# Softmax sums of a two-layer model: three quarters of the keys added by DMA onto the first quarter's weights, and one product with ones per head pair on four column tiles

## The reference, cut to what matters

```python
q = (x @ Wq + bq).reshape(B, S, H, DK)          # S = 512, H = 16, DK = 64
k = x @ Wk + bk
v = x @ Wv + bv
scores = jnp.einsum('bshd,btd->bhst', q, k) / np.sqrt(DK).astype(x.dtype)
w = jax.nn.softmax(scores, axis=-1)
out = jnp.einsum('bhst,btd->bshd', w, v).reshape(B, S, H * DV)
return out @ Wo + bo
```

## Time and profile before

| | us |
|---|---|
| median of 3 runs | 1349.38 |
| lowest, highest | 1345.81, 1350.87 |
| the profiled execution | 1346.94 |
| its span in the trace | 1345.2 |
| TensorE busy (matmul) | 1233.3 |
| VectorE busy | 1011.2 |
| ScalarE busy | 683.2 |
| GpSimd busy | 263.2 |

### The profile page before, as it was taken

The page is one execution under the profiler, slowest core; times in us unless marked ns, Lnnn a source line. Parts: engine busy times, 40 slices in busy tenths (PEclk is TensorE's granted clock), DMA queues, the critical chain, the costliest instruction groups (busy, mean ns, idle before and its releaser), DMA issues.

```text
span 1345.2 us, 21825 instructions
## 1 busy us (share of the span) xinstructions
PE 1233.3 (92%) x7185; PEld 725.0 (54%) x7185; DVE 1011.2 (75%) x2393; ACT 683.2 (51%) x1252; POOL 263.2 (20%) x314
## 2 busy tenths in 40 slices
PE   4559999999999999999999999999999989998997
PEld 2335445554555455555555555455555458785843
DVE  7776888578857885788588857886796767686775
ACT  3126545544554455444644464446444468685741
POOL 2033222200120012001200120012000206372640
PEclk9659999999999999999999999999999999998998
DMA  2062665122312231224222321232121457474461
GB/s 78 0 174 69 193 200 179 49 63 56 115 36 63 65 116 38 52 67 100 64 50 55 115 65 50 49 120 65 50 50 49 131 173 232 153 238 137 150 214 55
DMA packets 89779, 133.80 MB, mean 99 GB/s; under 512 B 33293, under 2 KB 49229, under 8 KB 85701
## 3 DMA queue, kind: packets, MB, share of 16 engines
q1 hardware_dynamic: 75108, 99.80, 26.2%
q0 software_dynamic: 11344, 31.64, 7.1%
q10 hardware_dynamic: 3216, 0.97, 0.3%
HBM read 59.86 MB, written 38.68 MB: 73 GB/s over the span
## 4 chain that ended last, share of the span: by engine, by line
PE 69%; DVE 19%; issue 4%; ACT 3%; SPq 3%; DMA 2%; POOL 1%; DVEq 0%; ACTq 0%; POOLq 0%
PE bank L1466 14%; PE bank L1438 7%; PE bank L1477 6%; PE bank L1392 6%; PE bank L1439 5%; PE bank L1297 4%; PE bank L1498 4%; PE bank L1299 4%; PE bank L1298 4%; DVE mneg L1029 4%; DVE q_lm L1021 3%; PE bank L1313 2%; PE bank L1348 2%; PE bank L1303 2%; PE bank L1356 1%
## 5 line engine op out<-in xcount | busy, mean ns | idle before, releaser
L846 ACT ACTIVATE wide<-bank 128x512 f32<-128x512 f32 x512 | 294.9, 598 | 338.2 <-PE bank L1439 337.8
L1029 DVE TENSOR_REDUCE mneg<-bank 128x1 f32<-128x512 f32 x512 | 329.7, 684 | 136.0 <-PE bank L1392 130.8
L1466 PE MATMUL bank<-wide,v_w 128*32 128x512 f32 x2048 | 246.2, 598 | 1.3 <-issue 1.0
L1438 PE MATMUL bank<-q_hh,k_hl 128*128 128x512 f32 x512 | 233.0, 455 | 11.3 <-ACT wide L846 11.3
L1439 PE MATMUL bank<-q_lm,k_h 65*128 65x512 f32 x512 | 203.1, 397 | 0.0
L1438 PEld LDWEIGHTS bank<-q_hh,k_hl 128*128 128x128 f32 x512 | 96.3, 188 | 131.6 <-issue 76.9
L636 POOL TENSOR_TENSOR rs<-rs,power 128x4 f32<-128x4 f32 x24 | 24.5, 1020 | 640.2 <-DVE rs L920 640.1
L1477 PE MATMUL bank<-wide,ones 128*32 128x512 f32 x992 | 129.1, 592 | 0.0
L708 POOL DMA_INDIRECT y_rows<-y_m,to_u x92 | 98.9, 1075 | 126.8 <-DVE y_m L1155 102.3
L1466 PEld LDWEIGHTS bank<-wide,v_w 128*32 128x32 f32 x2048 | 53.5, 109 | 121.0 <-issue 112.1
L1392 PE MATMUL bank<-k_b,q_x 128*128 128x512 f32 x256 | 104.4, 408 | 9.7 <-ACT qk L742 6.2
(11 more groups left out here) (238 smaller groups left out, 1969.8 us busy)
## 6 DMA issues: line engine op xcount, KB each, us to landing
q_hh<-q_x SPq DMA_DIRECT2D x256, 128.0 KB, 2.4
w_t<-w_rows SPq DMA_DIRECT2D x23, 1024.0 KB, 4.7
x_rows<-part_h POOLq DMA_DIRECT2D x65, 258.0 KB, 5.0
inv<-inverse_scratch SPq DMA_DIRECT2D x124, 128.0 KB, 2.9
w_rows<-w_t SPq DMA_DIRECT2D x8, 1024.0 KB, 5.0
x_m<-x_rows SPq DMA_DIRECT2D x23, 258.0 KB, 3.9
stage<-in_L_ffn_W SPq DMA_DIRECT2D x16, 256.0 KB, 5.0
yab<-y_rows POOLq DMA_DIRECT2D x8, 512.0 KB, 7.9
```

The source lines that it names most:

```text
L846: act.activation(wide[:, st.g % WIDE, :], ps, ACT.Exp, scale=SCALE1).then_inc(wide_full, 1)
L1029: dve.tensor_reduce(mneg[:, pair % 2, col:col + 1], ps[:], X, ALU.max, negate=True).then_inc(free, 1)
L1438: pe.matmul(ps, k_hl[:, n, t], q_hh[:, gh % HEADS, :], start=True, stop=False)
L1466: pe.matmul(ps_out[0][rows, :], v_w[:, n, c, TILE * d:TILE * d + TILE], weights, start=(c == 0), stop=(c == TT - 1))
```

## The change

Pairs 0 to 53 (`added(pair)`, `ADDED` = 54) form their sums in another way; pairs 54 to 63 stay as they were. For an added pair:

- ScalarE takes the exponential of the first key quarter twice, once into `wide` and once into a new buffer `total` (two buffers of both heads, 2 x 512 columns). The signal `wide_full` comes with the second.
- GpSimd issues three DMAs that add the slots of quarters 1, 2 and 3 (both heads, 128 x 1024 fp32, 512 KB) onto `total`. Each waits for the exponentials of its quarter and for the completion of the add before it.
- TensorE no longer multiplies the weights with ones. Instead `sum_of_added` runs four products of `ones` with 256 columns of `total`, one for each head and half of the queries on its own column tile, at the start of the next pair's first `values`.
- ScalarE may fill a slot of `wide` of quarters 1 to 3 again only once its add has landed, and `total` only once the pair two before has been summed.
- `sraw` is copied three steps later and over 256 columns only; the store of the sums, the reciprocal and the multiplication move two steps later (`SUM_LATER`), the second half of the output projection too (`WO_AT`). The addition L1209 goes.
- GpSimd's program is written along the steps: `root`, the adds, `split_expert`, the single scatters and the single zeroing DMAs each have a step number. Two of VectorE's cuts of layer 0 move (`L0_DVE`).
- `part_h` and `total` share their storage; `zeros` becomes a tensor of its own.

The diff, cut to its core:

```diff
+    ADDED = (NB - 1) * (H // 2) - 2
+    ADD_AT = {4: 1, 6: 2, 8: 3}
+    SUM_LATER = 2
+    WO_AT = [ATT - 10, ATT + 20]
...
-    L0_DVE = [-14, -11, -11, -10, -7, -6, -4, -2, 0, 0, 9, 10, 13, 17, 18, 21, 25, 26, 29, 30, 30, 31, 32,
-              34, 35, 37, 38, 39, 40, 42, 43, 44, 44]
+    L0_DVE = [-14, -13, -11, -10, -7, -6, -4, -2, 0, 0, 9, 10, 13, 17, 18, 21, 25, 26, 29, 30, 30, 32, 32,
+              34, 35, 37, 38, 39, 40, 42, 42, 44, 44]
...
+    ROOT_AT = [30, 42, 51]
+    SCATTER_AT = [[3, 5, 7, 9], [17, 19, 21, 23]]
+    ZERO_AT = [25 + 2 * e for e in range(E)]
...
+    def on_sum(st):
+        return st.kind == "o" and added(pair_of(st)) and head_at(st.k)[1] == 0
+    def adds_before(pair, c):
+        return (TT - 1) * pair + c
...
+            def add(pair, c):
+                g = ATT * (pair // (H // 2)) + PAIR * (pair % (H // 2))
+                pool.wait_ge(wide_full, g + 2 * c + 2)
+                if pair or c > 1:
+                    pool.wait_ge(add_done, adds_before(pair, c - 1) * 16)
+                i = wide_at[g + 2 * c]
+                pool.dma_start(total[:, pair % 2], wide[:, i:i + 2, :], accum_op=ALU.add).then_inc(add_done, 16)
...
+            for st in steps:
+                if st.kind != "o":
+                    continue
+                if st.r < NB - 2 and st.k in ROOT_AT or st.r == NB - 2 and st.k in ROOT_AT[0:2]:
                     root()
+                if add_event(st) is not None:
+                    add(*add_event(st))
+                if st.r == 0 and st.k in SPLIT_STEPS:
+                    split_expert(SPLIT_STEPS.index(st.k))
...
-                    if st.g >= WIDE:
-                        act.wait_ge(second_done, st.g - WIDE + 1)
+                    past = wide_before.get(st.g)
+                    if past is not None:
+                        act.wait_ge(second_done, past.g + 1)
+                        if past.kind == "o" and added(pair_of(past)) and not on_sum(past):
+                            act.wait_ge(add_done, adds_before(pair_of(past), head_at(past.k)[1]) * 16)
...
+                        ins = act.activation(wide[:, wide_at[st.g], :], ps, ACT.Exp, scale=SCALE1)
+                        if on_sum(st):
+                            if pair_of(st) >= 2:
+                                act.wait_ge(summed, pair_of(st) - 1)
+                            ins = act.activation(total[:, pair_of(st) % 2, st.k % 2, :], ps, ACT.Exp, scale=SCALE1)
+                        ins.then_inc(wide_full, 1)
...
+                pair = pair_end(st, 4)
+                if pair is not None and added(pair):
+                    act.wait_ge(summed, pair + 1)
+                    act.wait_ge(sums_stored[pair % 2], 16 * (pair // 2))
+                    act.activation(sraw[:, pair % 2, 0:S // 2], ps_out[1][:, 0:S // 2], ACT.Identity).then_inc(out_free[1], 1)
...
+            def sum_of_added(pair):
+                free_bank(("ps", pair))
+                pe.wait_ge(add_done, adds_before(pair, TT - 1) * 16)
+                for b in range(2):
+                    for h in range(2):
+                        rows, cols = slice(DK * b + TILE * h, DK * b + TILE * h + TILE), slice(S // 2 * h, S // 2 * h + S // 2)
+                        last = pe.matmul(ps_out[1][rows, 0:S // 2], ones[:], total[:, pair % 2, b, cols], start=True, stop=True)
+                last.then_inc(summed, 1)
...
                 if half == 0:
+                    if pair and added(pair - 1):
+                        sum_of_added(pair - 1)
+                    free_bank(("pv", pair))
...
+                        if added(pair):
+                            last.then_inc(second_done, 1)
+                if added(pair):
+                    return
```

More of the change, by code:

```diff
@@ L183, in pair_end, with add_event @@
         return past.r * (H // 2) + past.k // PAIR
+    def add_event(st):
+        if st.kind != "o":
+            return None
+        for at_, c in ADD_AT.items():
+            pair, s = divmod(ATT * st.r + st.k - at_, PAIR)
+            if s == 0 and 0 <= pair and added(pair):
+                return pair, c
+        return None
     def direct(pair):
@@ L241, in norm_at @@
     def norm_at(r):
-        at_ = dict(enumerate(NORM_AT))
+        at_ = {p: k + (SUM_LATER if added(r * (H // 2) + p) else 0) for p, k in enumerate(NORM_AT)}
         if r == NB - 1:
@@ L402, in two_layers @@
         lo_done, second_done = sem("lo_done"), sem("second_done")
+        add_done, summed = sem("add_done"), sem("summed")
         out_free = [sem(f"out_free{i}") for i in range(OUTB)]
@@ L508, in sums_and_inverses @@
                         continue
-                    if k == PAIR * p + 12:
+                    later = SUM_LATER if added(pair) else 0
+                    if k == PAIR * p + 12 + later:
                         emptied(sp, ("ps", pair))
@@ L518, in sums_and_inverses @@
                         sp.wait_ge(inverted, four)
-                        sp.dma_start(sums[:], scratch_s.rearrange("a g (p n) -> (g p) a n", p=32)).then_inc(sums_loaded, 16)
-                    if k == PAIR * p + 17 and p % 2 == 1:
+                        if added(pair):
+                            sp.dma_start(sums[:, 0, :], scratch_s[0].rearrange("g (p n) -> (g p) n", p=32)).then_inc(sums_loaded, 16)
+                        else:
+                            sp.dma_start(sums[:], scratch_s.rearrange("a g (p n) -> (g p) a n", p=32)).then_inc(sums_loaded, 16)
+                    if k == PAIR * p + 17 + later and p % 2 == 1:
                         for i in range(2):
@@ L655, in _, with zero, scatter @@
                     .then_inc(split_l, 1)
-            pool.memset(part_h[:].bitcast(F32), 0.0).then_inc(consts, 1)
+            pool.memset(zeros[:], 0.0).then_inc(consts, 1)
             pool.memset(k_a[:].bitcast(F32), 0.0).then_inc(consts, 1)
             pool.memset(k_b[:].bitcast(F32), 0.0).then_inc(consts, 1)
[L661 to L670, removed]
+            def zero(n, e):
+                pool.dma_start(x_rows[ZONE * e + S * n:ZONE * e + S * (n + 1), :].rearrange("(p i) c -> p (i c)", p=P),
+                               zeros[:]).then_inc(zeroed[n % 2], 16)
+            def scatter(n, b, i):
+                if i == 0:
                     if n or b:
@@ L678, in scatter, with split_expert @@
                         pool.wait_ge(routed, n + 1)
[L679 to L691, removed]
+                pool.indirect_dma_start(x_rows, bass.IndirectOffsetOnAxis(ap=slot_u[:, b, i:i + 1], axis=0),
+                                        xr[:, i, :], None).then_inc(scattered, 16)
+            def split_expert(j):
                 e, second = divmod(j, 2)
@@ L1206, in row_end @@
                     pair = r * (H // 2) + p
-                    if k == PAIR * p + 16 and not direct(pair):
+                    if k == PAIR * p + 16 + (SUM_LATER if added(pair) else 0) and not direct(pair):
                         dve.wait_ge(sums_loaded, 16 * (pair // 2 + 1))
-                        link(dve.tensor_tensor(sums[:, 0, :], sums[:, 0, :], sums[:, 1, :], ALU.add))
+                        if not added(pair):
+                            link(dve.tensor_tensor(sums[:, 0, :], sums[:, 0, :], sums[:, 1, :], ALU.add))
                         dve.reciprocal(sums[:, 0, :], sums[:, 0, :]).then_inc(inverted, 1)
@@ L1473, in values @@
                                 rows = slice(DK * b + TILE * d, DK * b + TILE * d + TILE)
-                                last = pe.matmul(ps_out[1][rows, :], ones[:], weights, start=(c == 0), stop=(c == TT - 1))
+                                last = pe.matmul(ps_out[1][rows, :], ones[:], weights_of(c, b), start=(c == 0), stop=(c == TT - 1))
                         else:
                             rows = slice(DK * b + TILE * (c % 2), DK * b + TILE * (c % 2) + TILE)
-                            last = pe.matmul(ps_out[1][rows, :], ones[:], weights, start=(half == 0), stop=(half == 1))
+                            last = pe.matmul(ps_out[1][rows, :], ones[:], weights_of(c, b), start=(half == 0), stop=(half == 1))
                         last.then_inc(second_done, 1)
```

95 lines of the change are left out of this document (66 added, 29 removed).

## The result

The changed kernel takes 1455.6 us (median of 4 runs, 1449.3 to 1462.6), the kernel before 1348.2: a ratio of 1.080 (1.074 to 1.085). It is 107 us slower, where 31 us faster was forecast. The number is that of rival A (1452 at L = 6.0); the mechanism, as the experiments show, is for the most part another.

The account below looks back on a forecast made before the run. TensorE, busy for 92% of the span, was taken as the bound. 1346.9 - 70.2 (TensorE) + 10.5 (VectorE) + 21 + 8 (adds) = 1316.2 us, as a median 1318; likeliest case 1300 to 1333, 8 in 10 within 1284 to 1400.

Parts of the forecast that it names:

- rival A: The adds in series bound nearly all pairs; slower from L of about 5.3, 1452 us at L = 6.0; chance 0.29.
- L: Time on GpSimd from one add's issue to the next one's; taken as 4.6 us, 5.2 in batch 0.
- What TensorE is rid of: TensorE loses two groups of products with ones and gains a half: net 1.30 us a pair, 70.2 us over the run.
- ScalarE's second exponential: Two more exponentials a pair on ScalarE, hidden in time; taken as even, bound 16 us either way.
- VectorE's 1.5 us a batch: VectorE, nearly full in the fourth and fifth pair, gives back some gain: 10.5 us for seven batches.
- The chain of adds: Three GpSimd adds in series per pair hold up light pairs: 21 us in batches 1 to 6, 8 in batch 0.
- The double pass: An add passes its data twice through the DMA engines: 1.7 + 3.2 = 4.9 us, against 3.3 priced as a copy.
- the prediction's own formula: A pair lasts at least 3L, nothing carried over between pairs; at 13.8 us, 3.5 us lost a batch.
- the prediction's own signs: In the profile after, A shows L above 5.3, batches over 137 us, ScalarE's add waits nearly everywhere, perhaps a lower clock.
- these adds are alone in their queue by construction: Reason for keeping L near 2.4 to 4.9 us, not the 7.9 of a DMA with seven like it around.
- 0.5 us for the others' traffic on the adds: Added to the middle price of 4.1 us for query copies and zeroing DMAs, giving 4.6 us an add.
- Batch 0: Higher DMA share and GpSimd's weight splitting there: adds at 5.2 us, four pairs lose 8 us together.

Follow-up runs that it names:

- The batch of 129.4 us: Changed kernel without the adding DMAs and their waits, reciprocal one step earlier and store of the inverses two steps earlier: 0.964 of before.
- old steps: Changed kernel without adds, sums at their steps before the change: 0.969 of before; with the adds' traffic in an unused buffer, batches 1 to 6: 1.019.
- early inverses: Reciprocal one step and store of the inverses two steps earlier than in the changed kernel: 1.060 of before with adds, 0.964 without.

## Why the prediction was wrong

- **What TensorE is rid of** (1.30 us a pair) was about right. The batch of 129.4 us against 137.0 is within 1.3 of 126.6 + 1.5. TensorE's busy time in it is 122.7; by the prediction 131.3 - 10.4 = 120.9. (In the changed kernel itself TensorE's busy time did not fall by 70 us but by 3; its products take longer at the lower clock.)
- **ScalarE's second exponential** at nothing and **VectorE's 1.5 us a batch** fit the same number: batches 1 to 6 took 46.0 us less than before, predicted 59.8 - 9 = 50.8. Neither was measured by itself. The whole gain of that kernel was 48 us, against the 60 of the terms; most of the difference is in batch 0.
- **The chain of adds** was sized too small and was still not the main point. L was taken as 4.6. The double pass, 4.9, is what the shortest interval shows (4.91), but the mean in batches 1 to 6 is 5.7. At 5.7 the prediction's own formula gives 17.5 us a batch, 105 in six. The series costs 20 there, and that 21 was predicted is luck: two errors that cancel, L too small and a formula that asks too much. Rival A uses the same formula, so its hit at L = 6.0 is luck of the same kind. By the prediction's own signs (L above 5.3, a batch above 137 us, a lower clock) the profile would be read as A; only the experiments part the two.
- **The step that failed** is the one that priced the adds by their series alone: "these adds are alone in their queue by construction", with 0.5 us for the others' traffic on the adds, and nothing for the adds' traffic on the others. 84.9 MB of adds, each at twice the engine time of a copy, raise the DMA share from 0.25 to about 0.7; the sums and the inverses take twice as long to land, and TensorE waits 51 us for the row of maxima. The traffic costs 66 to 72 us in batches 1 to 6. On the old steps it lengthens the light pairs (from 11.4 to 14.5 us and from 12.8 to 14.3, means of batches 2 to 5), though the fifth pair as well (17.7 to 20.8), and the two longest hardly; this is near the shape that rival A would give.
- **A second cost had no term at all**: the moved steps. The prediction took the shift of store, reciprocal and multiplication as one move that keeps its distances. It keeps them in steps, but not in microseconds and not in the order of SyncE's queue; which of the two costs more was not separated. Together they cost 34 us in batches 1 to 6 without adds, 27 with them.
- **Batch 0** was put at 8 us for the adds. With early inverses it is 150.5 against 126.7, 24 us, three times the term. L there was put at 5.2 and is 7.0 in the median. What share the traffic has in the 24 was not separated.

In all, batches 1 to 6: 762.9 (no adds, early inverses) + 72 (traffic) + 20 (series) + 27 (moved steps) = 882; before, 808.9. The terms are differences along one chain of kernels, so they must add up to the 881.6 of the changed kernel; the check is that the traffic came out at 66 and 72 by two ways, and the moved steps at 34 and 27. These 73 us and the 32 more in batch 0 are 105, near the 102 between the two spans.

No version with adds beat the kernel before. The kernels that did (0.964, 0.969, 0.988) leave the adds out and with them three quarters of the sums.

## What to carry to other kernels

A transfer has two prices: how late it comes, and how late it makes the others. For the second, list the small transfers whose landing a compute engine waits for, with the slack of each, before putting large ones beside them; here the raised DMA share alone cost as much as the change was to save. And when work is moved along a schedule written in steps, measure its slack in microseconds at the new place, and look at what stands ahead of it in its queue there: steps are not of one length.

## What was not expected of the hardware

- An adding DMA of 128 x 4 KB took 83.4 us of one DMA engine per MB, a copy of the same 42.2 (estimates from the queue's rows above); issuing it took GpSimd 0.88 us, the copy 0.55.
- Stores of 4 to 8 KB from SBUF to DRAM on SyncE's queue were waited for 3.0 us each instead of 1.5 while the adds ran on GpSimd's.
- Beside GpSimd's tensor_tensor with both inputs in SBUF, VectorE's took 1139 ns on average instead of 685.
- TensorE's mean granted clock was 1.00 in 750 us with 6% idle time and 0.96 with 9% (705.6 and 681.9 busy of 750). In one place it was 0.50 for 3.4 us right after TensorE had stood still for 4.6 us.
